# Two attention layers and two expert layers on one core: values of two pairs in one projection, two openings reordered

## The chip, the cores and the metric
The kernel runs on one NeuronCore of a Trainium2 chip. The metric is the device time of one execution in microseconds, the median of several runs. An execution has one launch, in which all four layers follow one another. TensorE multiplies into PSUM; VectorE (DVE), ScalarE (ACT) and GpSimd (POOL) do the rest; SyncE (SP) issues most DMAs. Each engine runs its own list of instructions in order and waits on semaphores.

## The reference
The input is x of 16 sequences of 256 rows of 128 numbers. Four steps follow, each with a residual and a layer normalisation:
```
x = layernorm(x + attention0(x))   # 16 heads of 64, scores masked half-causally: softmax(q k / 8) v, then Wo
x = layernorm(x + experts0(x))     # 8 experts, top two by a router, silu(x Wg) * (x Wu), then Wd
x = layernorm(x + attention1(x))   # keys and values through latents of 128, 16 heads of 8, rotary positions
x = layernorm(x + experts1(x))     # two shared experts and the top two of eight routed ones
```
In attention0, v = x Wv + bv with Wv of 128x1024; the bias of v is added behind the softmax product. All of it is in 32-bit floats.

## The kernel before
**Products of halves.** `split_mm` (L98 to L102) makes a product of two 32-bit tiles from a high half (an F32R copy) and a low half (the difference): high by high, low by high, high by low, three matmuls of one pass each. A plain 32-bit matmul takes several passes; two of them show as four rows.

**First attention** (`attention0`). A batch is one sequence; its transposed rows lie in `xt`, `xt_h` and `xt_l`. The 16 heads are taken as eight pairs, hp 0 to 7. TensorE's round for pair hp (L703 and on) is: transpose the scaled probabilities of hp (L710), make the scores of hp+2 (L646 to L652), multiply probabilities and values of hp (L735, L739), project queries and keys of hp+3 into the bank QK (`project_qk`, six products at L100 to L102), project the values of hp+3 into the bank VO (`project_v`, L638). VO also takes the output of L735, so a projection into it waits for ScalarE's eviction (L308). ScalarE makes the exponentials (L263), evicts the transposes (L300) and the outputs. VectorE takes the maxima (L455, L456), scales the second head's probabilities (L463 to L465), and evicts queries and keys (L444, L445) and values (L450). GpSimd scales the first head's (L370). Some rounds have more: hp 0 the output projection of the batch before (L660), hp 1 and 2 its normalisation, hp 3 to 7 its routing, hp 4 and 5 the transposes of the next input and their halves (L255, L258 on ScalarE, L440 on VectorE). Fourteen of the sixteen batches are one hardware loop; the first and the last are written apart. Scores wait for `qk_done` (L445 of their pair).

**First routed stage** (`routed0`). Blocks of 256 rows, sorted by expert, run in a pipeline from `steps`. ScalarE makes the high half of a block's gate and up weights (`weights_high`, L932) and of its input (`input_high`, L941), VectorE the low halves (L969, L974), TensorE the transposes of the rows (L901) and 24 products of halves a block. For block 0 the order on ScalarE is: input 0, weights 0, input 1, and weights 1 behind the first gate.

**Second attention** (`attention1`). Before its loop stands a long opening that makes keys, values, stacks of rotated queries and keys and the maxima of batch 0 and 1 (16 heads, L1467 and L2172 in turn). GpSimd weighs and adds the expert rows of a coming batch (`weigh_rows`: L1998, L2003, L2005), takes the power for the normalisation (L2010), and multiplies with the cosines (L1974, L1977, L1983). VectorE normalises (L2222), makes low halves (L2228), multiplies with the sines (L2128), adds (L2135), and makes the halves of the sums (L2136, L2141). TensorE makes latents, keys (L1443 to L1445), values (L1450), the turned key (L1455) and the stacks (L1460, L1461). In the opening GpSimd also splits the shared experts' weights (L2070, L2072), which are used only behind the last batch.

## Time and profile before
| | |
|---|---|
| median of 3 runs | 1431.57 us (1431.30 to 1431.68) |
| the profiled execution | 1433.0 us, its span 1431.4 us, mean granted clock 0.967 |
| TensorE busy | 1307.9 us, 91% of the span |
| VectorE, ScalarE, GpSimd busy | 1003.7, 937.5, 624.3 us |
| the span in 40 slices, TensorE | 6999999999999999939999947999999999788996 |
| granted clock in the slices | 9999999999999999969999967999999999998997 |

A digit is the busy share of a slice of 35.8 us in tenths. The first attention fills the slices up to 625 us, the first routed stage those up to 833 us, the second attention begins there. Each stage opens with a slice in which TensorE waits. Of TensorE's clock the profile gives the granted share: 1.00 is 2.4 GHz, 0.50 is 1.2 GHz. The rows' durations overlap, since instructions are pipelined; the distance of two starts is what one takes from its queue.

### The profile page before, as it was taken

The numbers are of one execution on the slowest core, as the hardware profiler recorded it, in microseconds if no ns is written. First come the engines' busy times: TensorE is split into PE (matmuls) and PEld (weight loads), VectorE is DVE, ScalarE is ACT, GpSimd is POOL, SyncE is SP. The second block draws the span as 40 slices with busy tenths as digits, with TensorE's granted clock in tenths as the row PEclk, the third lists the DMA queues.
The fourth block names the chain that finished last, engine by engine and source line by source line (L and its number), as shares of the span: only waits on it lengthen the run. The fifth ranks groups of instructions, "written<-read, shape, count | busy, mean of one in ns | idle before, by whom it ended". The sixth has DMA issues, their size and how long they took to land. (4 is left out here: it accounts for less than half of the span.)

```text
span 1431.4 us, 34641 instructions
## 1 busy us (share of the span) xinstructions
PE 1307.9 (91%) x10910; PEld 1096.2 (77%) x10911; DVE 1003.7 (70%) x3142; ACT 937.5 (65%) x2431; POOL 624.3 (44%) x978
## 2 busy tenths in 40 slices
PE   6999999999999999939999947999999999788996
PEld 5888888888888888739999936777777777567985
DVE  5777777777777777646666658898989897463443
ACT  4666666666666666525655536778787877576863
POOL 2243434443344333423434453355565643334773
PEclk9999999999999999969999967999999999998997
DMA  7111102020202020011111162212221400203325
GB/s 254 48 52 37 68 19 75 18 83 22 83 22 81 20 83 21 11 42 54 56 54 56 36 197 68 76 32 72 86 83 60 158 8 16 90 16 104 105 76 186
DMA packets 52087, 97.65 MB, mean 68 GB/s; under 512 B 10928, under 2 KB 42032, under 8 KB 49392
## 3 DMA queue, kind: packets, MB, share of 16 engines
q1 hardware_dynamic: 41488, 76.48, 16.9%
q0 software_dynamic: 9088, 18.89, 3.9%
q10 hardware_dynamic: 1440, 1.39, 0.3%
q8 instruction: 37, 0.61, 0.2%
q14 instruction: 34, 0.28, 0.1%
HBM read 75.75 MB, written 62.06 MB: 96 GB/s over the span
## 5 line engine op out<-in xcount | busy, mean ns | idle before, releaser
L370 POOL TENSOR_TENSOR a_prob<-a_prob,a_rl 128x128 f32<-128x128 f32 (+1 forms) x256 | 128.1, 520 | 291.4 <-DVE a_rl L461 291.3
L263 ACT ACTIVATE a_prob<-psum,a_nmx 128x128 f32<-128x128 f32 (+1 forms) x512 | 209.8, 419 | 18.4 <-DVE a_nmx L456 18.4
L2172 DVE TENSOR_REDUCE a_nmx<-psum 128x2 f32<-128x512 f32 x256 | 170.0, 685 | 21.5 <-PE psum L1467 18.4
L300 ACT ACTIVATE a_probt<-psum 128x768 f32<-128x768 f32 x128 | 103.8, 811 | 82.2 <-PE psum L710 82.2
L861 POOL DMA_INDIRECT yt<-m_yrow,m_dest x78 | 74.8, 959 | 130.8 <-ACT m_yrow L936 118.9
L1837 ACT ACTIVATE a_prob<-psum 128x1024 f32<-128x1024 f32 x128 | 127.3, 1023 | 6.4 <-PE psum L1497 6.2
L1467 PE MATMUL psum<-k_stk,a_q_stk 96*128 96x256 f32 x512 | 116.4, 320 | 14.5 <-DVE a_nmx L2172 10.6
L308 ACT ACTIVATE a_ot<-psum,a_bias 128x256 f32<-128x256 f32 x128 | 61.0, 476 | 97.5 <-PE psum L739 97.5
L710 PE MATMUL psum<-ident,a_prob 128*128 128x128 f32 x768 | 105.3, 273 | 14.3 <-DVE a_prob L465 14.3
L1467 PEld LDWEIGHTS psum<-k_stk,a_q_stk 96*128 96x128 f32 x512 | 78.5, 195 | 45.2 <-DVE a_nmx L2172 18.6
L455 DVE TENSOR_REDUCE a_nmx<-psum 128x2 f32<-128x256 f32 x128 | 54.2, 424 | 80.9 <-PE psum L652 80.9
L263 ACT ACTIVATION_READ_ACCUMULATOR a_prob<-psum,a_nmx 128x1 f32 x512 | 105.1, 205 | 0.0
L710 PEld LDWEIGHTS psum<-ident,a_prob 128*128 128x128 f32 x768 | 86.3, 141 | 16.9 <-issue 14.3
L963 DVE TENSOR_TENSOR m_hid<-m_act_out,psum 128x512 f32<-128x512 f32 x78 | 53.6, 687 | 64.5 <-PE psum L102 48.4
L100 PE MATMUL psum<-m_x_h,m_w_h 128*128 128x256 f32 x312 | 94.9, 304 | 1.9 <-DVE m_w_l L969 1.9
L1063 POOL DMA_INDIRECT yt<-m_yrow,m_dest x78 | 75.6, 969 | 41.0 <-issue 21.4
L100 PE MATMUL psum<-a_xt_h,a_wqk_h 128*128 128x256 f32 x256 | 86.1, 336 | 5.4 <-DVE a_xt_l L440 4.8
L102 PE MATMUL psum<-m_x_l,m_w_h 128*128 128x256 f32 x312 | 88.8, 285 | 0.0
L101 PE MATMUL psum<-m_x_h,m_w_l 128*128 128x256 f32 x312 | 88.7, 284 | 0.0
L456 DVE TENSOR_REDUCE a_nmx<-psum 128x2 f32<-128x512 f32 x128 | 87.1, 680 | 0.0
L735 PE MATMUL psum<-a_probt,a_v 128*64 128x256 f32 x512 | 83.5, 401 | 3.5 <-ACT a_probt L300 1.9
L1497 PE MATMUL psum<-a_q_stk,k_stk 128*128 128x256 f32 x512 | 86.5, 292 | 0.0
(350 smaller groups left out, 3911.5 us busy)
## 6 DMA issues: line engine op xcount, KB each, us to landing
xs<-in_fill SPq DMA_DIRECT2D x144, 264.0 KB, 4.1
m_xrow<-xs SPq DMA_DIRECT2D x78, 132.0 KB, 2.1
w<-in_w SPq DMA_DIRECT2D x16, 256.0 KB, 3.9
a_yin<-yt SPq DMA_DIRECT2D x16, 256.0 KB, 2.7
f_yin<-yt SPq DMA_DIRECT2D x7, 512.0 KB, 7.9
w<-in_wr SPq DMA_DIRECT2D x2, 1284.0 KB, 7.3
yt<-m_yrow,m_dest POOLq DMA_INDIRECT x156, 2.2
xs<-in_fill_idle SPq DMA_DIRECT2D x2, 1056.0 KB, 6.5
```

The costliest lines, as they stand in the source:

```text
L100: nc.tensor.matmul(out, wh, xh, start=start, stop=False)
L101: nc.tensor.matmul(out, wl, xh, start=False, stop=False)
L102: return nc.tensor.matmul(out, wh, xl, start=False, stop=stop)
L263: last = nc.scalar.activation(prob[:, slot, h, at], S[:, 2 * slot + h, at], ACT.Exp, bias=nmx[:, slot, q, h:h + 1], accum_out=lsum[:, slot ...
L300: nc.scalar.activation(probt[:, hp % 2], PT[:, :, 0:SW], ACT.Copy).then_inc(pt_done, 1)
L370: last = nc.gpsimd.tensor_tensor(prob[:, slot, 0, at], prob[:, slot, 0, at], rl[:, slot, 0, q:q + 1].to_broadcast(prob[:, slot, 0, at].sha ...
L456: nc.vector.reduce_max(nmx[:, slot, 1, :], S[:, 2 * slot:2 * slot + 2, P:SW], AX.X, negate=True).then_inc(nmx_done, 1)
L710: last = nc.tensor.transpose(PT[:, h, t * P:(t + 1) * P], prob[:, hp % 2, h, t * P:(t + 1) * P], g.ident[:])
L1467: last = nc.tensor.matmul(bank[:, q * T:(q + 1) * T], q_stk[0:KR, p, h // HG, q * P:(q + 1) * P], k_stk[p][0:KR, h, :], start=True, stop=True)
L1497: last = nc.tensor.matmul(out[:, k * T:(k + 1) * T], k_stk[p][:, h, k * P:(k + 1) * P], q_stk[:, p, h // HG, :], start=True, stop=True)
L1837: nc.scalar.activation(prob[:, k % 2, 2 * (t % 2):2 * (t % 2) + 2, :], ST[:, 2 * (t % 2):2 * (t % 2) + 2, :], ACT.Exp, scale=SCALE).then_i ...
L2172: nc.vector.reduce_max(nmx[:, :, h:h + 1], bank.rearrange("p (q k) -> p q k", q=QB), AX.X, negate=True).then_inc(mx_done, 1)
```

## The change
Four edits:
- **Values of two pairs.** `project_v` runs in every second round (odd hp) and projects pairs hp+3 and hp+4 at once, from halves: for each of the two row groups three products with 256 columns, into the whole of VO. VectorE's eviction takes both pairs in one copy, and stands in the odd rounds only. The value weights are split by GpSimd at the start, in two parts, and `xt` no longer goes into a product, so ScalarE's second copy of the input doesn't wait for the values.
- **First routed stage.** Weights 0 are split ahead of input 0; weights 1 behind input 1, ahead of the first gate.
- **Second attention's opening.** GpSimd's `weigh_rows(1)` waits for the first rows, `weigh_rows(2)` for the first rotated key; TensorE makes the turned key and the second latents ahead of the first values; VectorE rotates the key ahead of the values' eviction, and makes the low half of the first input ahead of the rotation matrix's copy, for which only the keys wait now.
- **Shared weights.** Their split moves from the opening into batch 0 and 1 of the second attention, one step at the end of each.

The diff, with unchanged lines left out:

```diff
@@ -125,6 +125,7 @@
     wv = sb("wv", [P, H0 * DK0])
+    wv_h, wv_l = sb("wv_h", [P, H0 * DK0], F32R), sb("wv_l", [P, H0 * DK0], F32R)
     wo = sb("wo", [P, HP, P])
@@ -182,6 +183,7 @@
     ntr_ps, nt_act, nt_done = sem("ntr_ps"), sem("nt_act"), sem("nt_done")
+    wv_high, wv_split = sem("wv_high"), sem("wv_split")
     init, dve_chain = sem("init"), sem("dve_chain")
@@ -250,11 +252,9 @@
 
-            def activations(n):
+            def activations():
 
                 nc.scalar.activation(halves(xt_h), TC, ACT.Copy).then_inc(xt_act, 1)
-                if n is not None:
-                    act.wait_ge(v_ps, n)
                 nc.scalar.activation(halves(xt), TC, ACT.Copy).then_inc(xt_act, 1)
@@ -267,7 +267,7 @@
             act.wait_ge(xtr_ps, 1)
-            activations(None)
+            activations()
             weights_high(1)
@@ -295,7 +295,7 @@
                         act.wait_ge(xtr_ps, i + 2)
-                        activations(i * HP + HP)
+                        activations()
                     act.wait_ge(pt_ps, s + 1)
@@ -321,6 +321,12 @@
             pool.wait_ge(init, 3)
+            pool.wait_ge(wv_in, 16)
+            for k, part in enumerate(parts):
+                whole = wv[:, part].shape
+                nc.gpsimd.tensor_tensor(wv_h[:, part], wv[:, part], one[:].to_broadcast(whole), ALU.mult).then_inc(wv_high, 1)
+                pool.wait_ge(wv_high, k + 1)
+                nc.gpsimd.tensor_tensor(wv_l[:, part], wv[:, part], wv_h[:, part].bitcast(F32), ALU.subtract).then_inc(wv_split, 1)
             pool.sem_inc(kept, 1)
@@ -447,7 +453,7 @@
                 dve.wait_ge(v_ps, n)
-                nc.vector.tensor_copy(v[:, hp % 4], VO[:, 0:QB * P].rearrange("p (q n) -> p q n", q=QB)
+                nc.vector.tensor_copy(v[:, hp % 4:hp % 4 + 2], VO.rearrange("p (q k n) -> p k q n", q=QB, k=2)
                                       ).then_inc(v_done, 1)
@@ -559,10 +565,9 @@
             evac_qk(1, 2)
-            evac_v(1, 2)
+            evac_v(2, 2)
             maxima(0, 1)
             evac_qk(2, 3)
-            evac_v(2, 3)
             maxima(1, 2)
@@ -593,7 +598,8 @@
                         evac_qk(hp + 3, s + 4)
-                        evac_v(hp + 3, s + 4)
+                        if hp % 2 == 1:
+                            evac_v(hp + 3, i * (HP // 2) + hp // 2 + 3)
                     if hp == 4 and not first:
@@ -633,10 +639,13 @@
             def project_v(hp):
+
                 hp = hp % HP
-                for q in range(QB):
-                    last = nc.tensor.matmul(VO[:, q * P:(q + 1) * P], xt[:, q * P:(q + 1) * P], wv[:, hp * P:(hp + 1) * P],
-                                            start=True, stop=True)
+                pairs = slice(hp * P, (hp + 2) * P)
+                for q in range(QB):
+                    at = slice(q * P, (q + 1) * P)
+                    last = split_mm(nc, VO[:, q * 2 * P:(q + 1) * 2 * P], xt_h[:, at], xt_l[:, at], wv_h[:, pairs], wv_l[:, pairs],
+                                    True, True)
                 last.then_inc(v_ps, 1)
@@ -681,15 +690,17 @@
             project_qk(0)
-            pe.wait_ge(wv_in, 16)
+            pe.wait_ge(wv_split, 1)
             project_v(0)
...
                 pe.wait_ge(qk_done, s + 1)
-                pe.wait_ge(v_done, s + 1)
                 project_qk(s + 1)
-                project_v(s + 1)
+                if s == 0:
+                    pe.wait_ge(v_done, 1)
+                    pe.wait_ge(wv_split, 2)
+                    project_v(2)
                 if s == 0:
@@ -724,10 +735,8 @@
                         output(i * HP + 1, y_ps)
-                    if not final or hp + 2 < HP:
-                        pe.wait_ge(v_done, s + 3)
-                    else:
-                        pe.wait_ge(ot_done, s + 1)
+                    pe.wait_ge(v_done, i * (HP // 2) + (min(hp, 4) if final else hp) // 2 + 2)
+                    pe.wait_ge(ot_done, s + 1)
                     pe.wait_ge(pt_done, s + 1)
@@ -765,8 +774,9 @@
                         rows_to_columns(xin, xtr_ps)
-                    pe.wait_ge(ot_done, s + 2)
-                    project_v(hp + 3)
+                    if hp % 2 == 1:
+                        pe.wait_ge(ot_done, s + 2)
+                        project_v(hp + 3)
 
@@ -943,7 +953,7 @@
                     gate(j, u, 0)
-                if looped or 0 <= j + 1 < NB:
+                if looped or 2 <= j + 1 < NB:
                     weights_high(j + 1, (u + 1) % SLOTS)
@@ -951,7 +961,10 @@
                     input_high(j + 2, (u + 2) % SLOTS)
-
+                if not looped and j == -1:
+                    weights_high(1, 1)
+
+            weights_high(0, 0)
             steps(act, step)
@@ -979,13 +992,16 @@
                     product(j, u, 0)
-                if looped or 0 <= j + 1 < NB:
+                if looped or 2 <= j + 1 < NB:
                     weights_low(j + 1, (u + 1) % SLOTS)
...
                     input_low(j + 2, (u + 2) % SLOTS)
-
+                if not looped and j == -1:
+                    weights_low(1, 1)
+
+            weights_low(0, 0)
             steps(dve, step)
@@ -1358,7 +1374,7 @@
                          "nrm_done", "ntr_ps", "nt_act", "nt_done"))
-    stage_in = sem("stage_in")
+    stage_in, ws_high = sem("stage_in"), sem("ws_high")
     y_in, filled = [sem("y_in0"), sem("y_in1")], sem("filled")
@@ -1565,17 +1581,19 @@
             pe.wait_ge(loaded, LOADS * 16)
-            pe.wait_ge(consts, 2)
+            pe.wait_ge(consts, 1)
             pe.wait_ge(rx_done, 1)
             latents(columns_of(0), 1)
+            pe.wait_ge(consts, 2)
             keys(columns_of(0), 1)
...
             pe.wait_ge(xsin_done, 1)
-            values(0)
             turn()
...
             latents(columns_of(1), 2, PV)
+            pe.wait_ge(ksin_done, 1)
+            values(0)
             pe.wait_ge(sel_done, 1)
@@ -2056,6 +2074,7 @@
             incoming_power(1)
+            pool.wait_ge(rows_done, 1)
             weigh_rows(1, 1, 16)
@@ -2064,16 +2083,13 @@
             rotate_x(columns_of(1), 2, 2)
+            pool.wait_ge(k_split, 1)
             weigh_rows(2, 0, 32)
             rotate_k(2)
-            pool.wait_ge(stage_in, 16)
-            nc.gpsimd.tensor_tensor(g.ws[:, 0, :], stage[:], one[:].to_broadcast([P, S1 * W1C]), ALU.mult).then_inc(pool_chain, 1)
-            pool.wait_ge(pool_chain, 3)
-            nc.gpsimd.tensor_tensor(g.ws[:, 1, :], stage[:], g.ws[:, 0, :].bitcast(F32), ALU.subtract)
             incoming_power(3)
...
             pool.wait_ge(rx_done, 3)
-            rotate_x(columns_of(2), 3, 4)
+            rotate_x(columns_of(2), 3, 3)
             rotate_k(3)
@@ -2095,10 +2111,20 @@
                         pool.wait_ge(rx_done, n + 4)
-                        rotate_x(columns_of(n + 3), n + 4, n + 5)
+                        rotate_x(columns_of(n + 3), n + 4, n + 4)
                         rotate_k(n + 4)
...
                         scatter_rows(half, n - 1, i * (E1 * 16) + 16)
+                    else:
+                        shared_weights(half)
+
+            def shared_weights(half):
+                if half == 0:
+                    pool.wait_ge(stage_in, 16)
+                    nc.gpsimd.tensor_tensor(g.ws[:, 0, :], stage[:], one[:].to_broadcast([P, S1 * W1C]), ALU.mult).then_inc(ws_high, 1)
+                else:
+                    pool.wait_ge(ws_high, 1)
+                    nc.gpsimd.tensor_tensor(g.ws[:, 1, :], stage[:], g.ws[:, 0, :].bitcast(F32), ALU.subtract)
 
@@ -2276,8 +2302,8 @@
             nc.vector.tensor_tensor(wd_l[:], small32[:, 0:2, :], wd_h[:].bitcast(F32), ALU.subtract).then_inc(consts, 1)
+            incoming_low(columns_of(0), 1)
             nc.vector.tensor_copy(rot[:], small32[:, 2, :]).then_inc(consts, 1)
-            incoming_low(columns_of(0), 1)
             incoming_variances(2)
@@ -2287,8 +2313,8 @@
             rotate_k_first(1)
+            rotate_k(1, True)
             values(0, 1)
-            rotate_k(1, True)
             stacks(1, 0, 1)
```

## Rows read from the trace of the kernel before

**Rows 1.** Windows: stretch, its length, busy us of each engine, PEclk, DMA share, GB/s.
```profile
29.00:597.00 568.00, 553.52 (x5100) 459.40 (x5098) 428.77 (x1502) 378.29 (x1308) 223.60 (x432) 1.00 0.15 48
...
625.40:638.60 13.20, 4.71 (x20) 3.96 (x21) 2.58 (x6) 4.65 (x6) 0.67 (x1) 0.50 0.35 91
...
833.50:853.60 20.10, 7.49 (x26) 5.93 (x26) 13.45 (x37) 7.36 (x9) 12.03 (x20) 0.50 0.91 289
...
863.00:886.00 23.00, 17.66 (x77) 14.98 (x78) 20.11 (x51) 11.62 (x22) 6.98 (x9) 0.63 0.32 106
```

**Rows 2.** Timeline, two looped rounds: start, us, engine, line, operation [idle before <-releaser].
```profile
200.86 0.61 PE L638 MATMUL psum<-a_wv,a_xt 128*128 128x128 f32 x4
...
201.30 0.82 PE L710 MATMUL psum<-ident,a_prob 128*128 128x128 f32 x6
...
202.05 0.49 PE L646 MATMUL psum<-a_qkt 64*128 64x128 f32 x4
...
213.70 0.49 PE L646 MATMUL psum<-a_qkt 64*128 64x128 f32 x4 [0.16 <-DVE a_qkt L445]
...
201.46 0.47 DVE L445 TENSOR_SCALAR a_qkt<-psum,a_bias 128x256 f32<-128x256 f32 x1
...
201.85 0.41 DVE L450 COPY a_v<-psum 128x256 f32<-128x256 f32 x1
```

**Rows 3.** Timeline, the scores of hp 3; ScalarE's input copy of hp 5.
```profile
217.70 0.49 PE L646 MATMUL psum<-a_qkt 64*128 64x128 f32 x4
...
216.89 0.47 DVE L445 TENSOR_SCALAR a_qkt<-psum,a_bias 128x256 f32<-128x256 f32 x1
...
225.78 0.38 ACT L258 ACTIVATE a_xt<-psum 128x256 f32<-128x256 f32 x1
```

**Rows 4.** Timeline, the weight loads of the transposes of hp 6.
```profile
230.33 0.64 PEld L710 LDWEIGHTS psum<-ident,a_prob 128*128 128x128 f32 x6 [0.91 <-issue]
```

**Rows 5.** Timeline of VectorE, opening; DMA issue: KB each, us from issue to landing.
```profile
8.54 0.42 DVE L440 TENSOR_TENSOR a_xt_l<-a_xt,a_xt_h 128x256 fp32r<-128x256 f32 x1
...
a_wv<-in_wv ACTq DMA_DIRECT2D x1, 512.0 KB, 5.7
```

**Rows 6.** Timeline, opening of the first routed stage, VectorE and TensorE.
```profile
632.45 0.42 DVE L974 TENSOR_TENSOR m_x_l<-psum,m_x_h 128x256 fp32r<-128x256 f32 x1 [7.27 <-ACT m_x_h L941]
...
633.87 1.23 DVE L969 TENSOR_TENSOR m_w_l<-w,m_w_h 128x1024 fp32r<-128x1024 f32 x1 [0.87 <-ACT m_w_h L932]
...
635.25 0.55 PE L100 MATMUL psum<-m_x_h,m_w_h 128*128 128x256 f32 x1 [1.56 <-DVE m_w_l L969]
...
640.34 0.36 PE L100 MATMUL psum<-m_x_h,m_w_h 128*128 128x256 f32 x1 [0.29 <-DVE m_w_l L969]
```

**Rows 7.** Timeline, opening of the second attention: TensorE, VectorE, GpSimd.
```profile
850.47 1.20 PE L1450 MATMUL psum<-a_wu,a_vlat 128*128 128x128 f32 x4 [0.74 <-DVEq L2129]
...
856.03 0.33 PE L1460 MATMUL psum<-a_qk_h,a_sel 128*96 128x256 f32 x1 [2.26 <-DVE a_qk_l L2141]
...
863.44 0.88 PE L1467 MATMUL psum<-k_stk,a_q_stk 96*128 96x256 f32 x4 [2.39 <-ACT a_q_stk L1823]
...
841.40 1.32 DVE L2222 TENSOR_SCALAR a_rows<-a_res,a_cmv,a_crstd 128x128 f32<-128x128 f32 x2 [0.84 <-POOL a_crstd L2010]
...
853.94 1.01 DVE L2136 CAST a_qk_h<-a_rk 128x256 fp32r<-128x256 f32 x1
...
860.66 1.28 DVE L2135 TENSOR_TENSOR a_rq<-a_xsin,a_xcos 128x256 f32<-128x256 f32 x1 [1.20 <-PE psum L1461]
...
861.97 2.33 DVE L2136 CAST a_qk_h<-a_rq 128x256 fp32r<-128x256 f32 x1
...
865.70 0.29 DVE L2136 CAST a_qk_h<-a_rk 128x256 fp32r<-128x256 f32 x1
...
866.37 1.28 DVE L2172 TENSOR_REDUCE a_nmx<-psum 128x2 f32<-128x512 f32 x2
...
861.74 2.41 POOL L2072 TENSOR_TENSOR ws<-a_stage,ws 128x1024 fp32r<-128x1024 f32 x1
```


## Prediction

> **What bounds the kernel now.** I read the time by stages first, first the page, then the windows of the stages [rows 1]. The first attention runs to about 625 us and is nearly all TensorE: from 29 to 597 us TensorE is busy for 553.5 of 568.0 us at full clock. The routed stage after it (638.6 to 833.5 us) is TensorE's too; its opening is not, and runs at the 1.2 GHz level (granted 0.50). The opening of the second attention (833.5 to 853.6 us) is a chain of small steps: TensorE 7.5 of 20.1 us, again at 0.50. The change touches these places and nothing behind about 930 us, where TensorE leads again, so what an opening gains should reach the end.
>
> Busy is not the same as bound. One round of the looped batch shows two chains of almost equal length [rows 2]. TensorE makes the queries and keys (six products, 0.117 us apart), the values (L638), the transposes (L710), then the scores (L646). Beside the values and the transposes VectorE empties queries and keys (L444, L445). L445 ends at 201.93; the scores start at 202.05. Where the scores wait for L445 they start 0.06 us after its end (L445 of that round ends at 213.65, they start at 213.70); where they wait for TensorE alone they start 0.20 us after the last transpose's start. So in a plain round L445's chain has 0.06 us of slack, no more.
>
> **First attention, the loop.** Removed: in every round the values' four passes, 0.44 us of TensorE's queue (200.86 to 201.30) [rows 2]. Added: in every odd round six products of 256 columns. The queries and keys are six products of that same form and 0.117 us apart, so 0.71 us. That is +0.27 us in a round that has them, -0.44 in one that hasn't: 0.17 us for two rounds if TensorE's queue were all that counts. It isn't, so I walked one batch round by round, with the later of the two chains each time. Rounds are named hp 0 to 7; the values of an odd round stand ahead of the transposes of the even round after it.
> - hp 0 and hp 4 have the long values ahead of them and no slack: +0.27 each.
> - hp 1: transposes could start 0.44 earlier, but the scores are held by L445, slack 0.06. The transposes' eviction (0.81 us on ScalarE) is now early, and it had been the last gate of the next product by 0.09 us. Together -0.16.
> - hp 2: the scores already waited for L445; the long values fill that gap, but the eviction of the transposes comes 0.26 later and passes its slack: +0.14.
> - hp 3: two transposes of rows stand between keys and values, so L445 (217.36) was ready 0.34 us before the scores (217.70) [rows 3]. This returns 0.28, the eviction 0.09: -0.37.
> - hp 5: the same slack, but ScalarE's two copies of the next input (L258, end 226.17 [rows 3]) end just ahead of the scores and gate them: -0.17.
> - hp 6: TensorE stood idle 0.91 us before these transposes, for VectorE's scaling of the probabilities (L465) [rows 4]. The long values fit in there at no cost; VectorE's queue, which is the chain here, is shorter by one eviction (0.33 us of issue) in hp 4, of which 0.15 is a gain over what is counted so far: -0.15.
> - hp 7: held by the probabilities again: -0.04.
> Sum: 0.27 - 0.16 + 0.14 - 0.37 + 0.27 - 0.17 - 0.15 - 0.04 = -0.21 us of a batch's 37.1; with 14 looped batches -2.9 us. First and last batch have only some of these slacks; I take 0. The one eviction for two pairs (L450, 0.41 us for 256 columns [rows 2]; 0.41 to 0.82 for 512) stands behind L445 and ahead of the maxima, where VectorE waited 0.3 to 1.0 us each round: no cost. What is queued behind it (the reciprocal, and POOL's scaling behind that) comes 0.3 us later and is wanted 1.5 us later.
> Bounds: if the saving of TensorE's queue were all that counts, 64 pairs times 0.17 is -11 us; if the no-value rounds returned nothing but the 0.09 of the eviction, +0.27 in three even rounds and -0.09 in four odd ones is +0.45 a batch, +6 us.
>
> **First attention, the opening.** Four new POOL products split the value weights. They land 5.7 us after their issue at 1.7 us, so POOL starts near 7.5 us; L440, which TensorE waits for, stands at 8.54 [rows 5]. POOL's and VectorE's operations on SBUF hinder each other in this trace [rows 7]: a cast of VectorE's took 2.33 us beside POOL and 0.29 alone. I expect L425 and L440 to come about 1.5 us later; against it, the second values leave the path of the second scores (0.5 us). I take +1.0 us, bounds -0.5 (no contention) and +3 (L440 behind the 768-column product too).
> The Trainium skill, SBUF — State Buffer, section Who interferes with whom, says that a VectorE instruction with two SBUF inputs and a GpSimd one that reads SBUF exclude each other for the whole instruction, whoever starts first. By that rule alone the upper bound would be the value; it speaks against this part of the change. By that rule, the 1.28 us of L2135, a sum of two SBUF tiles that ran while POOL made the shared weights' halves [rows 7], agrees.
>
> **First routed stage.** Now the high halves of the first weights (L932) come behind the first input on ScalarE, and TensorE waits 1.56 us for their low halves (L969, end 635.10) [rows 6]. Made first they need no input. The input's low half ends at 632.87; the transposes of the second input take TensorE from 633.02 to 633.5, and then the first block can start: 1.75 us earlier. The clock is at 0.50 until 638.6, and the block has 24 products at 0.213 us, 5.1 us, where before the last third ran at 0.12. If the clock rises at the same moment as before, the block ends at 638.6, the next transposes 0.2 later, and the second block starts at 638.85 instead of 640.34; its weights, which it waited for (0.29 us), are made earlier now as well. -1.5 us; -3 if the clock rises earlier by as much as the work does; -1.2 at least.
>
> **Second attention, the opening.** The walk, at half clock [rows 7]:
> - POOL's weighing of batch 1 waits for the first rows. VectorE's two subtractions there took 1.32 us beside it, 0.60 us in batch 1 alone: -0.7. With the low half of the input ahead of the rotation matrix's copy -0.4 more: latents at 843.9 for 845.0.
> - The turn is ahead of the values on TensorE (their four passes begin at 850.47 and take 1.0 us of its queue): -1.0 for the key's rotation. That rotation has VectorE's values behind it now (-0.35) and POOL's weighing held back until it is done; its cast took 1.01 us beside POOL, 0.29 alone. The stacks (L1460) could start 3 us before 856.03; TensorE's latents and values (0.85 us each half) let them start near 853.3, -2.7.
> - The stacks, on TensorE and ScalarE, may lose some of this at half clock (8 products at 0.213 for 0.12): the first scores at 861.2 for 863.4.
> - The shared weights' split leaves POOL (its subtraction alone took 2.41 us). Of VectorE's rotation beside it the sum took 1.28 us and the cast 2.33, where the cast of the next rotation took 0.29. So the maxima (L2172), which start at 866.37, 2.9 us behind the first scores, follow them at once: 861.9, -4.4.
> From there to about 882 us the order is the old one, shifted. The split is moved into batch 0, on POOL behind the keys' cosines, where POOL has nothing to do for longer than one of its two steps takes: 0, at most +1 if VectorE's sums meet it. I take -4.4; bounds -5.5 and -1.5 (the clock of the stretch 863 to 886, 0.63 on average [rows 1], falls to 0.5 throughout, and the first dense stretch behind it starts at half).
>
> **Sum.** +1.0 - 2.9 - 1.5 - 4.4 = -7.8 us on the profiled execution: span 1431.4, its own time 1433.0, so 1425.2. The median of the runs is 1431.57, 1.4 below that execution: 1423.8.
>
> **Rivals.** (a) The loop gives nothing back: the rounds without values are held by L445 whatever TensorE does, the long values are exposed. For it: the slack of 0.06 in hp 1 and 7 [rows 2]; against: slack and idle time that the trace shows [rows 3, 4]. +6 us for the loop; it makes the loop slower once the four rounds without values return less than 0.68 us together (what the even rounds lose above), and the kernel slower by 0.2% below 0.33 us, with +2 at the first opening and only -4 at the two others. At its end: 1435.6. Chance 0.08. (b) TensorE's queue is all: the gates slide with it. -11 in the loop, 1415.7. Against: L445 hangs on TensorE's own last key product. 0.10. (c) The second attention's opening is held by something else once POOL is out of the way (ScalarE's stacks and markers, or the clock): -1.5 there, and +2 at the first opening: 1427.7, 0.17; with the loop at zero as well it is 1430.6, within the limit: 0.10. (d) The change does what it says and the clock helps both openings: 1420, part of the forecast's range. Forecast (1419 to 1427): 0.55.
>
> **Chances.** Range 1417.5 to 1430.5: it leaves out (a), and (b) in the main. 0.2% is 2.9 us, about what a measurement of this kernel can tell from no change. Faster: 0.55 + 0.10 + 0.17 = 0.82; same 0.10; slower 0.08.
>
> **What would show it.** In the profile after: products of L638's place 0.117 us apart, six in odd rounds; a batch of 36.9 us for 37.1 (steps of the loop right; 36.3 is rival b, 37.6 rival a); transposes' idle of 0.9 us ahead of hp 6 filled; the first queries' product of the kernel later than 9.1 us (opening); the first routed product near 2.1 us behind the first transposes rather than 3.9; L2172's first at about 28.4 us behind the second attention's start (833.5) for 32.9, with no VectorE cast over 1 us before it. Wrong would be: a batch longer than 37.1, or the maxima's start followed by new waits that give it back before the first looped batch.

## Result and profile after

The changed kernel takes 1423.91 us, the median of 4 runs (1422.01 to 1424.28). The kernel before, run beside it, takes 1431.43 us (4 runs, 1430.82 to 1431.68). The ratio is 0.9936, its 95% interval 0.9921 to 0.9951: faster by 0.5% to 0.8%. The forecast was 1423.8 us. The profiled execution of the changed kernel took 1424.06 us, its span 1422.4, against a span of 1431.4 before.

Page of the changed kernel, part 1 (busy time of each engine):
```profile
PE 1300.8 (91%) x10782; PEld 1080.4 (76%) x10783; DVE 995.6 (70%) x3078; ACT 934.0 (66%) x2431; POOL 625.8 (44%) x982
```

Windows of the changed kernel (length, busy us of PE, PEld, DVE, ACT, POOL, then granted clock, DMA share, GB/s), the stretches that answer to [rows 1]:
```profile
29.00:597.00 568.00, 548.04 (x4978) 445.98 (x4978) 425.19 (x1444) 376.28 (x1310) 222.93 (x432) 1.00 0.15 49
625.40:636.70 11.30, 3.60 (x16) 3.23 (x17) 3.42 (x9) 3.61 (x5) 1.14 (x2) 0.50 0.35 96
831.30:851.30 20.00, 8.16 (x27) 5.84 (x27) 14.40 (x38) 8.10 (x11) 12.18 (x20) 0.50 0.85 279
861.00:884.00 23.00, 21.50 (x97) 18.34 (x97) 19.25 (x53) 12.08 (x25) 6.91 (x9) 0.61 0.31 106
```
TensorE does 5.5 us less in the first attention (548.04 for 553.52), and VectorE 3.6 us less. The two openings are still at 0.50, and the second one's work stands closer together.

Timeline of the changed kernel, first product of the values in an odd round, the transposes and the scores behind it, with VectorE's evictions beside them; these answer to [rows 2] (columns as there):
```profile
175.92 0.28 PE L100 MATMUL psum<-a_wv_h,a_xt_h 128*128 128x256 f32 x1
...
176.64 0.82 PE L721 MATMUL psum<-ident,a_prob 128*128 128x128 f32 x6
177.45 0.49 PE L655 MATMUL psum<-a_qkt 64*128 64x128 f32 x4
...
176.92 0.47 DVE L451 TENSOR_SCALAR a_qkt<-psum,a_bias 128x256 f32<-128x256 f32 x1
177.31 0.68 DVE L456 COPY a_v<-psum 128x512 f32<-128x512 f32 x1
```
The six products take 0.72 us from 175.92 to 176.64, 0.12 apart. The scores (L655) start at 177.45, 0.06 us behind the end of the keys' eviction (L451, 177.39), as in the rounds of the kernel before whose scores waited for it. The copy for two pairs takes 0.68 us.

Where the 8.9 us between the two profiled spans lie (us). The third column is the profiled pair; the last compares executions with the same clock, or the same opening, from the experiments below:

| stretch | forecast | changed less before | like for like |
|---|---|---|---|
| start to batch 1's first transposes (52.90, 54.07) | +1.0 | +1.17 | -0.7 to -1.1 |
| 14 looped batches (519.25, 518.32) | -2.9 | -0.93 | -1.4 |
| last batch (34.45, 34.07) | 0 | -0.38 | -0.4 |
| to the routed stage's first transposes (24.71, 25.62) | 0 | +0.91 | +0.5 |
| its opening, to the second block (9.03, 6.27) | -1.5 | -2.76 | -1.5, in the mean -2.1 |
| rest of that stage, to 833.59 and 831.61 | 0 | +0.01 | 0 |
| second attention's opening, to the first maxima (32.78, 28.28) | -4.4 | -4.50 | -4.5, in the mean -5.3 |
| from there to its last maxima (358.39, 358.85) | 0 to +1 | +0.46 | +0.5 |
| from there to the end (206.6, 203.7) | 0 | -2.9 | about 0 |

The sum of the forecast came out; not each of its terms did.

### The profile page after: what moved, and what is told of

Read it like the earlier page. It is cut to its first block and busy times, and to the rows that moved or that the text cites. A ratio compares the mean times of both kernels' runs of the same rounds, so it can differ in the third digit from the quotient of the medians.

```text
span 1422.4 us, 34439 instructions
## 1 busy us (share of the span) xinstructions
PE 1300.8 (91%) x10782; PEld 1080.4 (76%) x10783; DVE 995.6 (70%) x3078; ACT 934.0 (66%) x2431; POOL 625.8 (44%) x982
## 5 line engine op out<-in xcount | busy, mean ns | idle before, releaser
L721 PE MATMUL psum<-ident,a_prob 128*128 128x128 f32 x768 | 106.5, 275 | 13.4 <-DVE a_prob L471 13.3
L1483 PEld LDWEIGHTS psum<-k_stk,a_q_stk 96*128 96x128 f32 x512 | 79.5, 197 | 42.6 <-issue 18.4
L721 PEld LDWEIGHTS psum<-ident,a_prob 128*128 128x128 f32 x768 | 84.7, 141 | 21.3 <-issue 16.4
```

Source lines behind the costliest of these rows:

```text
L721: last = nc.tensor.transpose(PT[:, h, t * P:(t + 1) * P], prob[:, hp % 2, h, t * P:(t + 1) * P], g.ident[:])
L1483: last = nc.tensor.matmul(bank[:, q * T:(q + 1) * T], q_stk[0:KR, p, h // HG, q * P:(q + 1) * P], k_stk[p][0:KR, h, :], start=True, stop=True)
```

## Experiments

Each kernel was timed beside the kernel before. The first four were measured where the kernel before took 1479.83 us (30 runs, 1474.58 to 1485.40); their traces agree with those above up to 951 us and are slower only behind it, for a reason that I didn't follow. They are compared with that median. For the others the kernel before took 1432.47 (12 runs) and, for the last three, 1433.48 us (16 runs).

**The values alone (values_alone).** The change in `attention0` only.
```diff
-                    project_v(hp + 3)
+                    if hp % 2 == 1:
+                        pe.wait_ge(ot_done, s + 2)
+                        project_v(hp + 3)
...
+            pool.wait_ge(wv_in, 16)
+            for k, part in enumerate(parts):
```


> Only the first attention's part of the change. The steps of the prediction (long values exposed in hp 0 and 4, returned in hp 3 and 5): a looped batch of 36.9 us for 37.1, and with +1 us at the opening 1429.5 us, ratio 0.9987. After the profile of the changed kernel, where a looped batch takes 37.03 us: 14 x -0.06 = -0.8 us in the loop and +1.2 us until batch 1, so 1431.8 us, ratio 1.000. Rival (the loop gives nothing back): 1436 us, ratio 1.003. Rival (TensorE's queue is all): 1421 us, ratio 0.993.

Measured: 1478.72 us (12 runs), ratio 0.9995 (0.9982 to 1.0008). A looped batch takes 36.99 us. This part alone gives nothing that can be told from zero, and both rivals (1.003 and 0.993) lie outside the interval.

**The first routed opening alone (routed_opening_alone).**
```diff
+            weights_high(0, 0)
             steps(act, step)
...
+            weights_low(0, 0)
             steps(dve, step)
```


> Only the first routed stage's part. The prediction's step: first product 1.75 us earlier, second block 1.5 us earlier: 1430.0 us, ratio 0.999. The changed kernel's profile shows 2.8 us from the first transposes to the second block, with the clock up 1.84 us earlier. If the clock rises a fixed time behind the work, 2.8 us here too: 1428.7 us, ratio 0.998; if the moment of the rise is an accident of where the stage begins, 1.5 us here, since the stage begins where it did before.

Measured: 1476.16 us (12 runs), ratio 0.9977 (0.9962 to 0.9992). Timeline, TensorE: the first transposes of the stage, the first product, the second block's first product.
```profile
631.14 0.69 PE L901 MATMUL psum<-ident,m_xrow 128*128 128x128 f32 x2 [11.77 <-DMA m_xrow<-xs]
...
633.16 0.56 PE L100 MATMUL psum<-m_x_h,m_w_h 128*128 128x256 f32 x1
...
638.71 0.37 PE L100 MATMUL psum<-m_x_h,m_w_h 128*128 128x256 f32 x1
```
The first product stands 2.02 us behind the first transposes, where it stood 3.94 behind them (631.31 to 635.25 [rows 6]). The second block comes at 638.71 for 640.34. The clock rose at the same moment as before (638.7 for 638.6), so the block's 24 products ran almost wholly at half speed. The interval of the medians, -1.2 to -5.6 us, holds this. It is the case that the prediction took as its value: -1.5, measured relative to the first transposes 7.57 for 9.03, -1.46. The clock doesn't always rise there: from the first transposes to the second block it is 6.27 to 7.37 us in the eight other traces with the new opening, and 9.02, 9.02, 9.03 and 9.47 in the four with the old one, 2.1 us less between the means of all.

**The second attention's opening alone (second_opening_alone).** All edits of `attention1`, the shared weights' move with them.
```diff
+            pool.wait_ge(rows_done, 1)
             weigh_rows(1, 1, 16)
...
+            rotate_k(1, True)
             values(0, 1)
-            rotate_k(1, True)
```


> Only the second attention's opening (with the shared weights' split moved). The prediction's step: the maxima start 4.4 us earlier and nothing is given back: 1427.1 us, ratio 0.9969. Rival (ScalarE or the clock holds the opening, 1.5 us): 1430 us, ratio 0.999. The changed kernel's profile shows 2.9 us more gained behind the last maxima; if that belongs to this part (and not to where the clock's changes happen to fall), the ratio is 0.995.

Measured: 1475.18 us (12 runs), ratio 0.9967 (0.9951 to 0.9984). Behind the second attention's start the stacks stand at 19.57 us (22.44 before), the first maxima at 27.36 (32.78), the 49th (which the expectations call the 48th) at 89.95 (94.53). The stretch behind the last maxima takes 235.4 us, against 236.2 and 235.9 in routed_opening_alone and values_alone, which have the old code there: the 2.9 us of the profiled pair aren't this part's.

This kernel's first attention is that of the kernel before, instruction for instruction, and yet its batch 1 begins 2.95 us later. Windows of the same stretch, this kernel and then the kernel before:
```profile
21.40:28.10 6.70, 6.22 (x33) 4.65 (x34) 2.44 (x10) 2.90 (x11) 1.16 (x3) 0.50 0.92 298
```
```profile
21.40:28.10 6.70, 6.37 (x62) 5.08 (x62) 4.21 (x16) 4.51 (x15) 2.38 (x5) 1.00 0.80 262
```
From 21.4 to 28.1 us TensorE ran at 0.50 in one execution and at 1.00 in the other, with 33 matmuls done for 62. So a difference of 3 us at this place between two profiled executions says nothing about two kernels.

**Three products in every round (halves_each_round).** The changed kernel with one row group's products in each round instead of both in every second one.
```diff
                     project_qk(hp + 3)
+                    if hp % 2 == 0:
+                        pe.wait_ge(ot_done, s + 2)
+                        project_v(hp + 2, 1)
...
                     if hp % 2 == 1:
                         pe.wait_ge(ot_done, s + 2)
-                        project_v(hp + 3)
+                        project_v(hp + 3, 0)
```


> The changed kernel, but the six products for two pairs are spread: three of them (one row group) in every round, each evicted by its own copy of 256 columns. If a round's length is the longer of two chains (TensorE's queue, and L445's eviction behind the last key product), three products (0.35 us for 0.44) shorten rounds with slack and lengthen none: a looped batch of 36.4 us for 37.03, 8 us less than the changed kernel at best and 4 at least: about 1418 us, ratio to before 0.991. If TensorE's queue is all, no difference to the changed kernel (same products): ratio 0.9945. If the long copy was what cost, VectorE's queue gets 0.33 us longer in even rounds and it is slower than the changed kernel.

Measured: 1471.68 us (7 runs), ratio 0.9941 (0.9920 to 0.9963), and a looped batch of 36.99 us, as in the changed kernel. The expected 36.4 was a miss. Timeline, TensorE, the transposes and scores of hp 2, then the scores of hp 3:
```profile
175.87 0.82 PE L720 MATMUL psum<-ident,a_prob 128*128 128x128 f32 x6
176.97 0.49 PE L653 MATMUL psum<-a_qkt 64*128 64x128 f32 x4 [0.29 <-DVE a_qkt L451]
...
181.13 0.49 PE L653 MATMUL psum<-a_qkt 64*128 64x128 f32 x4 [0.17 <-ACT a_xr L281]
```
With shorter products ahead of them the transposes come earlier, and the scores then wait 0.29 us for L451. What TensorE's queue saves in one round is not taken in it. Against changed_again hp 0 and hp 4 are 0.27 and 0.33 us shorter, as the theory had it, but hp 3 and hp 5 are 0.29 and 0.30 longer. The last line, the scores of hp 3, shows why for hp 3: they wait for ScalarE's copies of the rows (L281), since three products now stand ahead of the rows' transposes that feed them. The theory had left out this third chain, as the prediction had.

**The changed kernel again (changed_again).** No edit.

> The changed kernel once more, beside the three others. Its looped batch is 37.03 us again, its second attention's maxima start 28.6 us behind the stage's first instruction. What can differ from the first execution is where the granted clock changes fall: if the 2.9 us that the first execution gained behind the last maxima are such an accident, the stretch from the last maxima to the end is not shorter than in the kernel before; if they are the change's, it is 2.9 us shorter again.

Measured: 1424.88 us (5 runs), ratio 0.9944 (0.9924 to 0.9963), a looped batch of 36.99 us, first maxima 27.71 us behind the second attention's start (28.28 in the first execution; the granted clock of the stage's first 28 us was 0.62 here and 0.56 there). The stretch behind the last maxima takes 204.3 us at 0.95 of the clock, 2.3 us less than the 206.6 before, so by this run alone it would look like the change's. copy_more_before, below, has the old code there and takes 204.2.

**The shared weights' split back in the opening (shared_weights_back).**
```diff
             rotate_k(2)
+            pool.wait_ge(stage_in, 16)
+            nc.gpsimd.tensor_tensor(g.ws[:, 0, :], stage[:], one[:].to_broadcast([P, S1 * W1C]), ALU.mult).then_inc(pool_chain, 1)
+            pool.wait_ge(pool_chain, 3)
+            nc.gpsimd.tensor_tensor(g.ws[:, 1, :], stage[:], g.ws[:, 0, :].bitcast(F32), ALU.subtract)
             incoming_power(3)
```


> The changed kernel with the shared weights' split back in the second attention's opening. If the split beside VectorE's rotation is what held the maxima (2.9 us of it in the kernel before), they start 2.5 to 3 us later than in the changed kernel, with casts and sums of over 1 us on VectorE again; if the waits and the order alone did it (GpSimd done with the split before the rotation begins), less than 1 us later. Against the changed kernel: +2.5 us, ratio +0.0018; rival: within +0.0005.

Measured: 1427.70 us (6 runs), ratio 0.9963 (0.9945 to 0.9982). Timeline, GpSimd and VectorE:
```profile
858.12 2.40 POOL L2092 TENSOR_TENSOR ws<-a_stage,ws 128x1024 fp32r<-128x1024 f32 x1
...
856.58 1.74 DVE L2155 TENSOR_TENSOR a_rk<-a_ksin,a_kcos 128x256 f32<-128x256 f32 x1 [0.15 <-DVE a_ksin L2148]
858.35 2.32 DVE L2156 CAST a_qk_h<-a_rk 128x256 fp32r<-128x256 f32 x1
```
The key's rotation takes 1.74 us and its cast 2.32; in the changed kernel, where nothing of GpSimd's runs beside them, they take 0.43 and 0.29 (at 857.63 and 858.09). The cast ends 0.15 us behind GpSimd's subtraction. The first maxima stand 30.19 us behind the stage's start, 2.5 us later than in changed_again, whose clock there is the same (0.62). At the 49th maxima 1.0 us of that is left (91.80 for 90.84), at the last 0.9 (388.18 for 387.27). So this move is worth 2.5 us at its place and, by the traces, about 1 us at the last maxima. The medians differ by 2.8 us (1427.70 for 1424.88), but each is known to some 2.7 us only.

**GpSimd's two new waits out (gpsimd_waits_out).**
```diff
-            pool.wait_ge(rows_done, 1)
             weigh_rows(1, 1, 16)
...
-            pool.wait_ge(k_split, 1)
             weigh_rows(2, 0, 32)
```


> The changed kernel without GpSimd's two new waits in the second attention's opening: it weighs rows of batch 1 and 2 beside VectorE's first rows and first rotated key again. If the two engines hinder each other as the kernel before shows, the first rows take 1.3 us for 0.65 and the rotation's halves 2.4 us for 1.3: stacks 1.5 to 1.8 us later, of which the maxima see 1 to 1.8. Rival (the waits only move the collision, since GpSimd's own chain comes later for the next rows): maxima within 0.3 us of the changed kernel's.

Measured: 1425.26 us (5 runs), ratio 0.9949 (0.9931 to 0.9966). Timeline, VectorE:
```profile
839.35 1.32 DVE L2246 TENSOR_SCALAR a_rows<-a_res,a_cmv,a_crstd 128x128 f32<-128x128 f32 x2 [0.84 <-POOL a_crstd L2028]
...
851.50 1.15 DVE L2165 TENSOR_TENSOR a_qk_l<-a_rk,a_qk_h 128x256 fp32r<-128x256 f32 x1
```
The subtractions take 1.32 us again for 0.60, and the low half of the key 1.15 for 0.43. The stacks come 20.92 us behind the start for 19.76, the first maxima 1.0 us later than in the changed kernel's first execution (the clock 0.56 in both) and 1.6 later than in changed_again, and 0.8 is left at the last maxima (388.08 for 387.27). The total of five runs can't tell 0.8 us.

**The same products in even rounds (values_even_rounds).**
```diff
-                        if hp % 2 == 1:
-                            evac_v(hp + 3, i * (HP // 2) + hp // 2 + 3)
+                        if hp % 2 == 0:
+                            evac_v(hp + 2, i * (HP // 2) + hp // 2 + 2)
...
+                    if hp % 2 == 0:
+                        pe.wait_ge(ot_done, s + 2)
+                        project_v(hp + 2)
...
-                    if hp % 2 == 1:
-                        pe.wait_ge(ot_done, s + 2)
-                        project_v(hp + 3)
```


> The changed kernel with the same six products for two pairs, but in the even rounds (pairs hp+2 and hp+3). Same work, same number of instructions. If the place decides (the prediction's walk: a long projection costs 0.27 us where no slack stands behind it, and a round without one returns only what L445, the scaling and ScalarE's copies leave), the long ones now meet rounds 1, 3, 5 and 7, and the idle time ahead of hp 6 stays unused: a looped batch of 37.5 us (37.2 to 37.8) for 37.03, +3 to +10 us. If TensorE's queue is all, 37.0 us and no difference.

Measured: 1442.01 us (5 runs), ratio 1.0062 (1.0043 to 1.0081). A looped batch takes 38.15 us, 1.16 more than in the changed kernel; the expected 37.5 was too little. Timeline, TensorE, around the transposes of hp 3:
```profile
185.82 0.38 PE L629 MATMUL psum<-ident,a_nrm 128*128 128x128 f32 x2
186.03 0.82 PE L718 MATMUL psum<-ident,a_prob 128*128 128x128 f32 x6
187.03 0.49 PE L654 MATMUL psum<-a_qkt 64*128 64x128 f32 x4 [0.17 <-ACT a_xr L281]
```
Here the six products stand ahead of the transposes of the rows (L629), which feed ScalarE's two copies (L280, L281), for which the scores of hp 3 wait. The scores start 1.00 us behind the round's transposes; in [rows 2] it is 0.75. From scores to scores, hp 3 and hp 5 are 0.50 us each longer than in the kernel before and hp 1 and hp 7 0.26; against the changed kernel it is 0.63 and 0.65, 0.32 and 0.27, with 0.32 and 0.33 returned in hp 0 and hp 4. The same work in the neighbouring rounds costs 17 us (1442.01 for 1424.88).

**One copy more in hp 3, in the changed kernel and in the one before (copy_more_after, copy_more_before).** ScalarE copies the transposed rows once more into a tile that nothing reads.
```diff
                 act.wait_ge(ntr_ps, n)
+                nc.scalar.activation(halves(spare), TC, ACT.Copy)
                 nc.scalar.activation(halves(xr_h), TC, ACT.Copy).then_inc(nt_act, 1)
```


> The changed kernel with one more copy of the transposed rows on ScalarE (256 columns into a tile that nothing reads), ahead of the two that the scores of hp 3 wait for; such a copy is 0.27 us from the next one's start. Theory (since the changed loop was traced): in hp 3 the scores are held by the chain transposes of the rows, then ScalarE's copies, because the values no longer stand behind those transposes. Then hp 3 grows by the whole copy, its period from 4.26 to about 4.5 us, and the batch from 37.0 to about 37.25 us, 1428 us in all. Rival: VectorE's eviction of the keys or TensorE's queue holds them; then the copy has 0.1 us or more of slack and the batch grows by under 0.1 us.

> The kernel before with the same one more copy. In its hp 3 the copies end 0.28 us ahead of the scores (0.47 against 0.75 us behind the round's first transpose), since the values stand between the rows' transposes and the round's. Theory: most of the copy is hidden, hp 3 grows by 0 to 0.12 us and the batch stays within 37.1 to 37.2 us. Rival (the copies are no nearer to being the gate in the changed kernel than here): both kernels grow by the same amount.

Measured: 1429.61 us (8 runs, ratio 0.9971, 0.9956 to 0.9986) and 1433.33 us (8 runs, ratio 1.0000, 0.9984 to 1.0017). The looped batch takes 37.27 us for 36.99 in the changed kernel, +0.28, and 37.10 for 37.09 in the one before, +0.015. Timelines of hp 3 (L721, L723 and L712 are the round's transposes, L281 and L283 the second copy of the rows): the changed kernel, then with one copy more, then the kernel before with one copy more.
```profile
180.35 0.85 PE L721 MATMUL psum<-ident,a_prob 128*128 128x128 f32 x6
...
180.66 0.48 DVE L451 TENSOR_SCALAR a_qkt<-psum,a_bias 128x256 f32<-128x256 f32 x1
...
180.78 0.40 ACT L281 ACTIVATE a_xr<-psum 128x256 f32<-128x256 f32 x1
...
181.31 0.49 PE L655 MATMUL psum<-a_qkt 64*128 64x128 f32 x4
```
```profile
181.60 0.85 PE L723 MATMUL psum<-ident,a_prob 128*128 128x128 f32 x6
...
182.30 0.41 ACT L283 ACTIVATE a_xr<-psum 128x256 f32<-128x256 f32 x1
...
182.84 0.49 PE L657 MATMUL psum<-a_qkt 64*128 64x128 f32 x4 [0.39 <-ACT a_xr L283]
```
```profile
183.32 0.82 PE L712 MATMUL psum<-ident,a_prob 128*128 128x128 f32 x6
...
183.65 0.41 ACT L283 ACTIVATE a_xr<-psum 128x256 f32<-128x256 f32 x1
...
184.19 0.49 PE L648 MATMUL psum<-a_qkt 64*128 64x128 f32 x4
```
In the changed kernel the second copy ends at 181.18 and the scores start at 181.31; one copy more moves both by its whole 0.27 us against the round's transposes (1.24 us from transposes to scores for 0.96). In the kernel before hp 3 grows by 0.12 us, and hp 4 gives 0.10 of it back. Its scores then start 0.13 us behind the copy's end too, so the copies had 0.15 us of slack there, not the 0.28 that the distance to the scores suggests. The theory holds.

**The values ahead of the turn again (values_before_turn).**
```diff
             pe.wait_ge(xsin_done, 1)
+            values(0)
             turn()
...
-            pe.wait_ge(ksin_done, 1)
-            values(0)
             pe.wait_ge(sel_done, 1)
```


> The changed kernel with the second attention's values ahead of the key's turn on TensorE again, as in the kernel before. My prediction gave the turn's place 1.0 us of the key's rotation (four passes at half clock). Theory: the keys' stacks start about 1 us later behind the second attention's start (20.7 us for 19.7), the first maxima 0.5 to 1 us later (28.8 to 29.3 for 28.3), and at most 0.5 us of it is left at the 48th maxima (90.8). Rival (TensorE's own work before the stacks, not the rotation, is the gate): the stacks stay at 19.7.

Measured: 1425.44 us (3 runs), ratio 0.9936 (0.9914 to 0.9959). Timeline, TensorE:
```profile
848.41 1.20 PE L1466 MATMUL psum<-a_wu,a_vlat 128*128 128x128 f32 x4 [0.30 <-DVEq L2154]
...
852.78 0.50 PE L1476 MATMUL psum<-a_qk_h,a_sel 128*96 128x256 f32 x1 [1.04 <-DVE a_qk_l L2166]
```
The stacks begin 19.92 us behind the start for 19.69 and 19.76, the first maxima at 28.60 for 28.28 and 27.71, the last at 387.56 for 387.13 and 387.27. Of the first maxima only the 28.28 has the same clock (0.56; 27.71 has 0.62). The stacks stay nearly where they were, as the rival had it: the order of the turn is worth 0.2 to 0.4 us, not 1.0. The gate is not TensorE's own work, though. In the row above the stacks wait 1.04 us for the low half of the key.

## Why the prediction was right, and where its terms were not

**The loop: right sign, half the size.** The steps can be set against the trace by the time from the scores of one pair to those of the next (medians of 14 batches, us, changed_again less before; the profiled execution of the changed kernel gives the same within 0.05):

| | hp 0 | hp 1 | hp 2 | hp 3 | hp 4 | hp 5 | hp 6 | hp 7 | batch |
|---|---|---|---|---|---|---|---|---|---|
| forecast | +0.27 | -0.16 | +0.14 | -0.37 | +0.27 | -0.17 | -0.15 | -0.04 | -0.21 |
| measured | +0.26 | -0.06 | 0.00 | -0.13 | +0.17 | -0.16 | -0.17 | -0.01 | -0.10 |

Hp 0, 5, 6 and 7 are right within 0.03. Hp 1 and 2 are off by 0.10 and 0.14 and cancel to 0.04 together, which is luck. The step that failed is hp 3. It counted L445's slack of 0.34 us as free to take. But in the kernel before the values stood between the transposes of the rows and those of the round, and covered ScalarE's two copies of these rows. Without the values the copies are the last gate. I had seen that gate in hp 5 and not in hp 3. One copy more of 0.27 us in hp 3 cost 0.28 a batch in the changed kernel and 0.015 in the one before: that the copies are the gate is shown, not argued. Their slack before, 0.15 us, is about what hp 3 returned, 0.13. How much they cost is an estimate from rows. The keys' eviction (L451) ends at 181.14 there, and where scores wait for it they start 0.06 us later, so without the copies they could have started at 181.20 for 181.31; over 14 batches that is 1.5 us, the size of the loop's miss. It is half of hp 3's own miss of 0.24; of the other half hp 4 returns 0.10, and no run says where it comes from. Hp 3 and hp 4 together make +0.04 where the forecast had -0.10; this 0.14 is the whole miss and a little more. Over 14 batches the loop gave -1.4 us (36.99 for 37.09), in the profiled execution -0.9, for -2.9. Rival (a), 37.6 a batch, and rival (b), 36.3 (37.1 less four times 0.17 is 36.4), are both refuted; halves_each_round and values_even_rounds show why (b) could not hold: three or six products of the same length cost or save by what stands behind them.

**The last batch**, taken at 0, gave -0.4 us (34.07 and 34.06 for 34.45). In five of the thirteen executions, of old and new code, it took 1.5 us or more longer (35.7 to 36.9), at 0.95 of the clock for 1.00. The way from there to the routed stage gave it back: from the last transposes to the routed stage's first ones it is 24.55 to 24.83 us in the four traces with the old first attention and 24.67 to 25.62 in the seven with the new one, +0.5 between their means (24.69, 25.17). The routed transposes wait for a DMA of the rows there (11.74 us in the changed kernel); what holds that DMA back I didn't follow.

**The first opening: the mechanism was there, the sign of the sum was not.** Timeline of the changed kernel, GpSimd, VectorE and TensorE, to be read against [rows 5]:
```profile
8.54 1.05 POOL L329 TENSOR_TENSOR a_wv_l<-a_wv,a_wv_h 128x256 fp32r<-128x256 f32 x1
...
8.93 0.94 DVE L446 TENSOR_TENSOR a_xt_l<-a_xt,a_xt_h 128x256 fp32r<-128x256 f32 x1
...
10.02 0.55 PE L100 MATMUL psum<-a_xt_h,a_wqk_h 128*128 128x256 f32 x1 [5.69 <-DVE a_xt_l L446]
15.55 0.49 PE L655 MATMUL psum<-a_qkt 64*128 64x128 f32 x4
...
21.09 0.85 PE L721 MATMUL psum<-ident,a_prob 128*128 128x128 f32 x6 [2.59 <-DVE a_prob L471]
```
VectorE's low half of the input (L446) takes 0.94 us for 0.42 beside GpSimd's L329, and the first product comes at 10.02 for 9.10, +0.92. The forecast had about 1.5 for this step, less 0.5 for the second values. L446 takes 0.94 us in all nine traces with GpSimd's new products; the first product stands at 9.11 to 10.51 in them, 9.9 in the mean, and at 9.01 to 9.25 in the four without. The Trainium skill (SBUF — State Buffer, Who interferes with whom) has it that the second of the two blocks until the first is through; the trace agrees in kind: L446 ends at 9.87, 0.28 us behind the end of L329. But the first transposes of the probabilities come at 21.09 for 21.68, 0.6 us earlier. I had given 0.5 us for the second values' leaving this path; 1.5 came back. The first maxima are 0.44 us late (16.95 for 16.51), so 0.5 is back by then; the other 1.0 comes between them and the transposes, where VectorE now copies no third values ahead of the second maxima (0.41 us before, at 18.63).

Part of it is the clock, which the prediction left out here. Timeline of the kernel before, its first scores and VectorE behind its first maxima:
```profile
14.60 0.80 PE L646 MATMUL psum<-a_qkt 64*128 64x128 f32 x4
...
17.83 0.48 DVE L444 TENSOR_SCALAR a_qkt<-psum,a_bias 128x256 f32<-128x256 f32 x1 [0.30 <-PE psum L102]
```
The first scores (L646, L655 in the changed kernel) take 0.80 us before and 0.49 after: the first stretch with a granted clock of 1.00 begins at 15.5 us in the changed kernel, just ahead of them, and at 17.4 us in the one before, behind them (its products stand 0.21 us apart up to there and 0.12 behind it). Their maxima follow 1.40 us behind them for 1.91, and VectorE's wait of 0.30 us for the next product is gone. In all nine traces with the new products the clock first rises at 12.7 to 15.5 us, in the four without at 17.4 to 18.4. Why it rises earlier, and how the 1.5 us divide between the clock and the order of work, no run separates.

Then the clock fell again in some executions, and the sum can't be read from one pair. Start of batch 1 in the profiled executions with one of these two first openings, by the mean granted clock of the stretch from 17 to 30 us:

| | 1.00 | 0.87 | 0.74 |
|---|---|---|---|
| opening of the kernel before | 52.90, 52.93 | | 55.85, 56.24 |
| opening of the changed kernel | 52.21 | 54.07, 54.20, 54.57 | 54.45, 54.85, 55.52 |

In like columns the changed opening is 0.7 to 1.1 us earlier in the mean. The clock fell in 6 executions of 7 with it (and in halves_each_round and values_even_rounds, whose openings differ a little from both), and in 2 of 4 with the old one: too few to say that the change makes this likelier. If it does, that takes back what the opening gives; this stays open. values_alone can't tell: its terms add up to about -2.2 us of 1479 (-0.9, -1.4, -0.4 and the +0.5 above), and its interval is -2.7 to +1.2 us. The sign of this term is the step of the forecast that came out the other way: GpSimd's cost was seen, the return behind it was sized at a third. The Trainium skill says of a kernel's start (TensorE: Matmul & The Clock Gate, Part 1) that the number of matmuls at the low clock varies between runs of one kernel; the traces agree, with the first rise at 12.7 to 15.5 us in runs of one opening. The later fall is priced by second_opening_alone, at about 3 us.

**The routed opening: right.** Timeline of the changed kernel, VectorE and TensorE, against [rows 6]:
```profile
631.09 1.22 DVE L982 TENSOR_TENSOR m_w_l<-w,m_w_h 128x1024 fp32r<-128x1024 f32 x1 [5.14 <-ACT m_w_h L942]
633.21 0.42 DVE L987 TENSOR_TENSOR m_x_l<-psum,m_x_h 128x256 fp32r<-128x256 f32 x1 [0.90 <-ACT m_x_h L951]
...
632.08 0.69 PE L911 MATMUL psum<-ident,m_xrow 128*128 128x128 f32 x2 [11.74 <-DMA m_xrow<-xs]
633.78 0.66 PE L911 MATMUL psum<-ident,m_xrow 128*128 128x128 f32 x2 [1.02 <-DVE m_x_l L987]
634.10 0.56 PE L100 MATMUL psum<-m_x_h,m_w_h 128*128 128x256 f32 x1
...
638.35 0.36 PE L100 MATMUL psum<-m_x_h,m_w_h 128*128 128x256 f32 x1
```
The low weights are done at 632.31, before the input's low half (633.63); the second transposes take TensorE from 633.78, and the first product follows at 634.10, 2.02 us behind the first transposes. The forecast was near 2.1. The 24 products end earlier than forecast because here the clock rose at 636.75 and not at 638.6: -2.76 relative to the first transposes, within the forecast's "-3 if the clock rises earlier". With the clock as before it is -1.46 (routed_opening_alone), for -1.5. Over all traces it is -2.1 in the mean, so the value was at the cautious end of a range whose other end was forecast too.

**The second attention's opening: the mechanism right, the 0.1 us luck.** Timeline of the changed kernel, VectorE and TensorE, against [rows 7]:
```profile
839.30 0.60 DVE L2248 TENSOR_SCALAR a_rows<-a_res,a_cmv,a_crstd 128x128 f32<-128x128 f32 x2 [0.84 <-POOL a_crstd L2028]
...
849.99 0.70 DVE L2162 CAST a_qk_h<-a_rk 128x256 fp32r<-128x256 f32 x1
...
858.09 0.29 DVE L2162 CAST a_qk_h<-a_rk 128x256 fp32r<-128x256 f32 x1
...
859.89 1.29 DVE L2198 TENSOR_REDUCE a_nmx<-psum 128x2 f32<-128x512 f32 x2 [1.05 <-PE psum L1483]
...
851.30 0.50 PE L1476 MATMUL psum<-a_qk_h,a_sel 128*96 128x256 f32 x1
...
859.06 1.22 PE L1483 MATMUL psum<-k_stk,a_q_stk 96*128 96x256 f32 x4 [2.65 <-ACT a_q_stk L1841]
```
Behind the stage's start the forecast had 10.3, 19.7, 27.6 and 28.3 us for latents, stacks, first scores and first maxima. Measured were 10.19, 19.69, 27.45 and 28.28. The subtractions take 0.60 us for 1.32; the casts 0.29, and one 0.70, beside a product of GpSimd's; and the maxima follow the scores by 0.83 us for 2.93. That the profiled pair meets the forecast within 0.1 us is partly luck. The first maxima stand 27.36 to 28.28 us behind the start in the six executions with this opening, and 32.77 to 33.23 in the four with the old one: -4.5 to -5.9 us, -5.3 between the means, with the clock's share in it. And one term was mis-sized: the turn ahead of the values is worth 0.2 to 0.4 us, not 1.0, since the stacks then wait for the low half of the key all the same (values_before_turn, where they wait 1.04 us for it). GpSimd's two waits are worth 1.2 us at the stacks. Of the 4.5 us, 0.46 are given back by the last maxima; of the shared weights' part alone 1.6 of 2.5. "What an opening gains should reach the end" holds for the larger part of the whole and for less than half of this one. Rival (c) is refuted.

**What the sum owes to chance.** The last stretch (from the last maxima on) was 2.9 us shorter in the profiled execution, without any forecast. The kernel before with one copy more has that stretch unchanged in its code. Windows from the last maxima to the end: before, with one copy more, changed:
```profile
1224.77:1431.30 206.53, 177.23 (x1086) 147.50 (x1086) 89.07 (x343) 133.93 (x310) 108.20 (x124) 0.93 0.32 99
```
```profile
1231.67:1435.90 204.23, 174.72 (x1086) 144.94 (x1086) 88.52 (x343) 133.86 (x310) 107.70 (x124) 0.96 0.32 100
```
```profile
1218.74:1422.40 203.66, 174.50 (x1086) 144.58 (x1086) 88.51 (x343) 133.91 (x310) 108.02 (x124) 0.96 0.32 100
```
The old code took 204.2 us in another execution, at 0.96 of the clock; at 0.93 it took 206.5. So at least 2.3 of the 2.9 us are that one execution's clock and not the change; the other way about, the new code took 206.3 us at 0.94 in values_even_rounds. In the profiled pair this, and 1.3 us of clock in the routed opening, outweighed the 2.0 us that the loop didn't give, the 0.9 on the way to the routed stage and the 0.5 given back behind the second opening. By like executions the terms are -0.9, -1.4, -0.4, +0.5, -1.5 and -4.0, together -7.7 us; the medians differ by 7.5 here and 7.6 us for the kernel run again (-3.7, -4.7 us and -1.1 for the three parts alone, together -9.4, each with an interval of some 2 us to either side). With the means of all executions for the two later openings (-2.1, and -4.5 at the last maxima) the sum is -8.8, still inside the interval of the medians (-11.3 to -7.0). The forecast's -7.8 came out with other weights: less of the loop, more of the first opening. Its mechanisms held in the loop's other rounds and in both later openings; that the sum fits this closely is luck.

## What to carry to other kernels

Slack against the gate that you see is not yet a gain: when work is taken out of an in-order queue, ask what else it covered, and follow every wait of the next consumer, not the last one alone. Moving products of the same total length between neighbouring rounds was worth 17 us, removing 5.5 us of them 1.4. In an opening that is a chain of small steps, keep GpSimd's work on SBUF away from VectorE's steps on the chain; taking the two things out of each other's way was worth 2.5 and 1.0 us of the 4.5 at their place, and about 1.7 us at the last maxima. An in-order loop has more than two chains: lengthening one suspected step by a known amount, in both kernels, shows which of them is the gate and how much slack it had.

## What the runs showed of the hardware

- Two executions of the same instructions (the kernel before and second_opening_alone) differed by 3 us in the first 53 us, by a stretch at 0.50 of the clock that one had and the other hadn't, and two of the old code (before, copy_more_before) by 2.3 us in the last 206 (0.93 for 0.96). Differences of single profiled executions under 3 us at an opening need a like execution beside them.
- VectorE beside a product of GpSimd's on SBUF: a cast of 256 columns 2.32 us for 0.29, a subtraction 0.94 for 0.42, another 1.15 for 0.43, a sum 1.74 for 0.43; the cast ended 0.15 us behind GpSimd's instruction, the first subtraction 0.28 us behind it.
- TensorE first came to full clock 12.7 to 15.5 us behind the start in nine traces with the new products of the value weights, and 17.4 to 18.4 us in four without.
- Scores started 0.06 us behind the end of the VectorE instruction that they waited for, and 0.13 us behind the end of a ScalarE one (hp 3).
- An eviction of 512 columns from PSUM took VectorE 0.68 us, one of 256 columns 0.41.
